# Gate and up products of layer 0's expert blocks as three rounded passes instead of one fp32 product

## The reference

```
combine = top-2 scores of the router, normed, zero for the other experts
for e in range(16):
    h = silu(flat @ Wu[e]) * (flat @ Wg[e])      # 256 -> 128
    out = out + combine[:, e:e+1] * (h @ Wd[e])  # 128 -> 256
out = out + silu(flat @ Su) * (flat @ Sg) @ Sd   # shared
```

## Time and profile before

| | us |
|---|---|
| median of 3 runs | 1170.13 |
| lowest, highest | 1168.87, 1175.76 |
| profiled execution | 1172.08 |
| its span, first to last instruction | 1169.5 |
| busy in the span: PE, DVE, ACT, POOL | 899.2, 685.6, 467.1, 621.2 |
| layer 0's dispatch, about | 297 to 364 |
| layer 0's 47 blocks, about | 364 to 452 |
| re-load and add of layer 0's results, about | 452 to 476 |

### The profile page before, as it was taken

One profiled execution on the slowest core, in us unless ns is written; L12 is line 12 of the kernel. 1 busy time (PEld: TensorE's weight loads), 2 busy tenths in 40 slices (PEclk: granted clock), 3 DMA queues, 4 the chain that ended last, 5 costly groups with the idle time before them and its releaser, 6 DMA issues.

```text
span 1169.5 us, 22075 instructions
## 1 busy us (share of the span) xinstructions
PE 899.2 (77%) x5927; PEld 691.8 (59%) x5927; DVE 685.6 (59%) x2692; ACT 467.1 (40%) x1176; POOL 621.2 (53%) x870
## 2 busy tenths in 40 slices
PE   1687989878597992379987888856899999989900
PEld 1465667657355881256665565533688887778700
DVE  4678888865532554467687674352455544444568
ACT  2346666743112441257655443311344444444400
POOL 3646666523163652336558888755356655545500
PEclk9859999988798996559989576787999999999955
DMA  8500000000624543400002222566455655545287
GB/s 231 192 2 1 2 2 1 1 2 1 263 106 127 152 130 120 144 1 2 2 29 86 85 97 101 210 222 221 147 163 174 182 157 161 153 141 156 70 327 319
DMA packets 73093, 136.97 MB, mean 117 GB/s; under 512 B 13406, under 2 KB 51725, under 8 KB 70928
## 3 DMA queue, kind: packets, MB, share of 16 engines
q1 hardware_dynamic: 52144, 85.15, 22.8%
q0 software_dynamic: 17632, 46.73, 11.2%
q10 hardware_dynamic: 3200, 3.70, 0.9%
HBM read 79.15 MB, written 62.39 MB: 121 GB/s over the span
## 4 chain that ended last, share of the span: by engine, by line
PE 36%; DVE 9%; POOL 6%; issue 5%; ACT 2%; another core or an unknown queue 1%; DMA 1%; DVEq 0%; POOLq 0%; ACTq 0%; SPq 0%
PE s_psum L1996 12%; PE s_psum L2009 6%; PE s_psum L1988 3%; POOL rows L1553 3%; PE s_psum L1477 3%; PE s_psum L2004 2%; DVE a_masked L1074 2%; DVE f_rows L2096 2%; DVE f_xT L2096 2%; PE s_psum L549 1%; POOL a_probs L1414 1%; PE s_psum L1496 1%; PE s_psum L646 1%; PE s_psum L602 1%
## 5 line engine op out<-in xcount | busy, mean ns | idle before, releaser
L2106 POOL DMA_INDIRECT parts<-e_y,e_dest x206 | 202.7, 984 | 180.7 <-DVE e_y L2079 96.9
L1996 PE MATMUL s_psum<-wres,e_xT 128*128 x824 | 213.9, 382 | 1.8 <-ACT e_xT L2036 1.0
L1996 PEld LDWEIGHTS s_psum<-wres,e_xT 128*128 128x128 f32 x824 | 156.1, 191 | 26.1 <-issue 5.4
L1414 POOL TENSOR_SCALAR_AFFINE_SELECT a_probs<-a_probs 128x256 f32<-128x256 f32 x256 | 107.5, 444 | 117.6 <-ACT a_probs L870 116.8
L1553 POOL DMA_INDIRECT rows<-f_rows,f_place_at x128 | 125.2, 978 | 40.3 <-issue 31.7
L2009 PE MATMUL s_psum<-wres,e_hT 128*128 x412 | 125.3, 386 | 12.2 <-ACT e_hT L2046 11.6
L870 ACT ACTIVATE a_probs<-s_psum 128x768 f32<-128x768 f32 x128 | 104.6, 817 | 72.8 <-PE s_psum L629 68.2
L2041 ACT ACTIVATE e_act_out<-s_psum 128x128 f32<-128x128 f32 x206 | 57.1, 277 | 180.8 <-PE s_psum L1996 101.6
L2070 DVE TENSOR_TENSOR e_hid<-e_act_out,s_psum 128x128 f32<-128x128 f32 x206 | 59.0, 286 | 91.8 <-issue 42.6
L1074 DVE CUSTOM_DVE_ANT_0 a_masked<-s_psum,a_ahead 128x128 f32<-128x128 f32 (+1 forms) x256 | 76.1, 353 | 42.0 <-PE s_psum L605 39.1
L2079 DVE TENSOR_SCALAR e_y<-s_psum,e_xg 128x256 f32<-128x256 f32 x206 | 99.6, 484 | 0.7 <-issue 0.7
(11 more groups left out here) (297 smaller groups left out, 1993.4 us busy)
## 6 DMA issues: line engine op xcount, KB each, us to landing
e_xg<-rows SPq DMA_DIRECT2D x159, 160.0 KB
f_rows<-parts SPq DMA_DIRECT2D x8, 1024.0 KB, 7.2
f_xT<-parts SPq DMA_DIRECT2D x8, 1024.0 KB, 7.4
wres<-in_experts SPq DMA_DIRECT2D x21, 384.0 KB
e_xg<-rows SPq DMA_DIRECT2D x47, 144.0 KB
wres<-in_experts SPq DMA_DIRECT2D x4, 1536.0 KB
rows<-empty SPq DMA_DIRECT2D x1, 5120.0 KB, 24.1
e_yk<-parts SPq DMA_DIRECT2D x16, 256.0 KB, 2.9
```

Of the source, the lines that this page charges most:

```text
L1414: last = nc.gpsimd.affine_select(out=diagonal[:, :, a], in_=diagonal[:, :, a], compare_op=ALU.is_ge, fill=0.0, base=0, pattern=[[0, 2], [1 ...
L1996: last = nc.tensor.matmul(ps_u[b % 2][:, 0:2 * P], xT[b % 2][:, c * P:(c + 1) * P], wres[:, ds(e, 1), 2 * c * P:2 * (c + 1) * P].rearrange ...
L2106: nc.gpsimd.indirect_dma_start(out=parts[:, :], out_offset=bass.IndirectOffsetOnAxis(ap=dest[b % NY][:], axis=0), in_=y[b % NY][:], in_off ...
```

## The change

It applies to layer 0 alone (`front is None`); layer 1's blocks keep their fp32 products.

- ScalarE rounds each quarter of the gate and up weights to fp32r (`up_hi`) after the Silu of shared units 0 to 3. VectorE subtracts this from the weights, in place in `wres` (`up_lo`), after the adds of units 0 to 3. TensorE's blocks wait for the four subtractions instead of the four transfers.
- ScalarE's copy `xT` is now rounded to fp32r. VectorE writes the remainder `xT_lo` from PSUM and `xT`, one more instruction a block.
- TensorE computes the gate and up product as three products of rounded parts, high with high, high with low, low with high, for each half of the width: six matmuls for two.
- The gathered rows and the results lie in the buffer from which the rows were scattered (`m_rows`) instead of buffers of their own.

```
+    up_hi = sb("up_hi", [P, E, D], F32R)
+    up_lo = wres[:, :, 0:D].bitcast(F32R)
...
 # dispatch, scalar
             nc.scalar.activation(act_out[i % 2][:], ps_a[i % 2][:], ACT.Silu).then_inc(act_done, 1)
+            if i < 4:
+                act.wait_ge(quarter_loaded[i], 16)
+                nc.scalar.activation(up_hi[:, parts4[i]], wres[:, parts4[i], 0:D], ACT.Copy).then_inc(up_hi_done, 1)
...
 # dispatch, vector, after the add of unit i
+            if i < 4:
+                dve.wait_ge(up_hi_done, i + 1)
+                nc.vector.tensor_tensor(up_lo[:, parts4[i]], wres[:, parts4[i], 0:D], up_hi[:, parts4[i]].bitcast(F32),
+                                        ALU.subtract).then_inc(up_lo_done, 1)
...
 # expert_blocks
+        if split:
+            sent = begun["rows"][:].rearrange("p t n -> p (t n)")
+            xg = [sent[:, i * RW:(i + 1) * RW] for i in range(NX)]
+            y = [sent[:, NX * RW + i * H:NX * RW + (i + 1) * H] for i in range(NY)]
...
             def up(b, e):
                 pe.wait_ge(xT_done, b + 1)
                 wait(pe, hid_done, b - 1)
+                if split:
+                    pe.wait_ge(xT_lo_done, b + 1)
+                    n = 0
+                    for c in range(FC):
+                        for rows_part, w in split_passes(xT[b % 2], xT_lo[b % 2], up_hi, up_lo):
+                            last = nc.tensor.matmul(ps_u[b % 2][:, 0:2 * P], rows_part[:, c * P:(c + 1) * P],
+                                                    w[:, ds(e, 1), 2 * c * P:2 * (c + 1) * P].rearrange("p a n -> p (a n)"),
+                                                    start=n == 0, stop=n == 3 * FC - 1)
+                            n += 1
+                    last.then_inc(u_ps, 1)
+                    return
...
+            def keep_x_lo(b):
+                dve.wait_ge(xT_done, b + 1)
+                wait(dve, u_ps, b - 1)
+                nc.vector.tensor_tensor(xT_lo[b % 2][:], ps_x[b % 2][:, 0:H], xT[b % 2][:].bitcast(F32),
+                                        ALU.subtract).then_inc(xT_lo_done, 1)
...
                     multiply(i)
+                if split and i + 2 < NB:
+                    keep_x_lo(i + 2)
```

More of the change, by code:

```diff
@@ L1602, in dispatch @@
     hid = [sb(f"hid{i}", [P, BLK]) for i in range(2)]
+    up_hi = sb("up_hi", [P, E, D], F32R)
+    up_lo = wres[:, :, 0:D].bitcast(F32R)
+    parts4 = [slice(q * E // 4, (q + 1) * E // 4) for q in range(4)]
     ps_a, ps_b = [psum[:, i] for i in range(2)], [psum[:, 2 + i] for i in range(2)]
@@ L1629, in dispatch @@
     chain = Chain(sem("chain"), 1000)
-    front = {"wres_loaded": wres_loaded, "wres_count": 64, "tab_done": tab_done, "scattered": scattered}
+    quarter_loaded = [sem(f"quarter_loaded{q}") for q in range(4)]
+    up_hi_done = sem("up_hi_done")
+    up_lo_done = sem("up_lo_done")
+    front = {"wres_loaded": up_lo_done, "wres_count": 4, "tab_done": tab_done, "scattered": scattered, "up_hi": up_hi,
+             "up_lo": up_lo, "rows": X}
     @block.sync
@@ L1634, in _ @@
         sp.dma_start(ws[:], w_shared.rearrange("h p n -> p h n")).then_inc(shared_loaded, 16)
-        for q in range(4):
-            part = slice(q * E // 4, (q + 1) * E // 4)
-            sp.dma_start(wres[:, part], w_all[part].rearrange("e p n -> p e n")).then_inc(wres_loaded, 16)
+        for part, landed in zip(parts4, quarter_loaded):
+            sp.dma_start(wres[:, part], w_all[part].rearrange("e p n -> p e n")).then_inc(landed, 16)
     @block.gpsimd
@@ L1930, in expert_blocks @@
         dest = [sb(f"dest{i}", [P, 1], I32) for i in range(NY)]
-        xT = [sb(f"xT{i}", [P, H]) for i in range(2)]
+        split = front is None
+        xT = [sb(f"xT{i}", [P, H], F32R if split else F32) for i in range(2)]
+        if split:
+            xT_lo = [sb(f"xT_lo{i}", [P, H], F32R) for i in range(2)]
+            up_hi, up_lo = begun["up_hi"], begun["up_lo"]
         act_out = [sb(f"act_out{i}", [P, P]) for i in range(2)]
@@ L1934, in expert_blocks @@
         hT = [sb(f"hT{i}", [P, P]) for i in range(2)]
-        y = [sb(f"y{i}", [P, H]) for i in range(NY)]
-        xg = [sb(f"xg{i}", [P, RW]) for i in range(NX)]
+        if split:
+            sent = begun["rows"][:].rearrange("p t n -> p (t n)")
+            xg = [sent[:, i * RW:(i + 1) * RW] for i in range(NX)]
+            y = [sent[:, NX * RW + i * H:NX * RW + (i + 1) * H] for i in range(NY)]
+        else:
+            y = [sb(f"y{i}", [P, H]) for i in range(NY)]
+            xg = [sb(f"xg{i}", [P, RW]) for i in range(NX)]
         if front is None:
@@ L1947, in expert_blocks @@
         xT_done = sem("xT_done")
+        xT_lo_done = sem("xT_lo_done")
         u_ps = sem("u_ps")
@@ L1985, in turn @@
                 loaded(pe, b)
+                if split:
+                    wait(pe, xT_lo_done, b - 1)
                 wait(pe, xT_done, b - 1)
@@ L2083, in _ @@
             dve.wait_ge(begun["tab_done"], 1)
+            if split:
+                keep_x_lo(0)
+                keep_x_lo(1)
             for i in range(NB + 2):
```

## The result

| | before | change |
|---|---|---|
| median, us | 1169.76 | 1187.93 |
| lowest, highest (4 runs each) | 1168.87, 1175.76 | 1181.91, 1191.51 |
| profiled execution; span | 1172.08; 1169.5 | 1187.08; 1185.3 |
| first to last of the 32 dispatch scatters | 42.9 | 49.3 |
| stretch of the blocks: first transposes to last weighed tile, layer 0 | 83.6 | 92.7 |

The table has one run of the kernel before more than the three of the earlier table; a stretch runs to the start of the last weighed tile. The change is slower: ratio 1.0175, 95% interval 1.0128 to 1.0222. The prediction (1169.4, range to 1178) was wrong. Its step on the dispatch scatters held up; its gain of 7 us in the blocks became a loss of 9.

A forecast was written before the change was run, and what follows sets the result against it. GpSimd's scatters were taken to set the time before layer 0's blocks, TensorE within them. Terms -7.2 + 0.3 + 6.2 = -0.7 us gave a median of 1169.4 us, range 1162 to 1178.

The forecast's parts named there:

- Gate and up products, -7.2 us: Layer 0's blocks: six single-pass matmuls take 0.714 instead of 0.866 us, 0.152 less a block, times 47 blocks.
- on the path: Layer 0's blocks: TensorE paces them, so the 7.2 us saved in gate and up products shortens the kernel.
- under 1.473: Layer 0's blocks: GpSimd's 1.30 us a scatter (0.98 plus 0.32 between) fits the new block period of 1.473 us.
- the 0.05 for other surprises: Rival on the whole kernel: matmuls not single-pass here, or other surprises such as idle time falling elsewhere; chance 0.05.
- Low part of the rows on VectorE, hidden: Layer 0's blocks: one more VectorE instruction, 0.42 us, hides in 0.43 and 0.28 us of waiting; first block +0.3 us.
- rival 3: Layer 0's blocks: VectorE paces them, period near 1.6 us, result 1175.4, or 1196.6 at the upper bound; chance 0.12.
- rival 2: Layer 0's blocks: TensorE's queue, slowed by address-setting instructions, becomes the bound; +4.1 instead of -7.2, result 1180.7 us; chance 0.08.
- Held scatters, +6.2: Dispatch before layer 0's blocks: each of four VectorE weight subtractions holds one GpSimd scatter, 1.55 us each; ends 0 and 8.8.
- the mean of 1.55: Dispatch: assumed hold per scatter in us, between 2.2 if it starts just inside a subtraction and 0.9 if one slipped through.
- Rival 1: Dispatch: scatters are not held, and blocks start when TensorE finishes the shared units at 366.4; result 1165.1 us; chance 0.25.
- Units of the shared expert, hidden: Before layer 0's blocks: TensorE starts 0.9 us late four times, units end at 366.4, hidden before first transposes at 370.7.
- Shared buffers, nothing: Layer 0: gathered rows and results in the old row buffer cost nothing, with same sizes and its scatters already waited for.

The follow-up runs named there:

- e16: Kernel before plus a GpSimd write of 128x464 zeros behind every result scatter of both layers' blocks; ratio 0.9909 to the kernel before, layer 0 stretch 80.8 us.
- e15: Blocks' half of the change alone, on unrounded loaded weights, with a result scatter for only every second block of layer 0; layer 0 stretch 73.6 us.
- e2_blocks: Blocks' half of the change alone: six fp32r matmuls and rows' remainders on the loaded weights, own buffers; ratio 1.0045 to the kernel before, layer 0 stretch 90.1 us.
- e5: Blocks' half of the change alone, without layer 0's result scatters, plain DMAs writing the results at the end; layer 0 stretch 73.4 us.
- e1_dispatch: Dispatch half of the change alone: weights rounded and subtracted, shared buffers, blocks still fp32 without remainders; ratio 1.0055 to the kernel before, layer 0 stretch 83.5 us.
- e4_wider: The change with each of the six matmuls 320 columns wide instead of 256; ratio 1.0118 to the kernel before, layer 0 stretch 86.0 us.
- e13: Kernel before plus a GpSimd write of 128x576 zeros behind every result scatter of both layers' blocks; ratio 1.0120 to the kernel before, layer 0 stretch 84.8 us.
- e14: The change plus a GpSimd write of 128x576 zeros behind every result scatter; ratio 1.0157 to the kernel before, layer 0 stretch 84.7 us.
- e17: The change plus a GpSimd write of 128x464 zeros behind every result scatter; ratio 0.9970 to the kernel before, layer 0 stretch 80.8 us.

## Why the prediction was wrong

- **Gate and up products, -7.2 us: the arithmetic right, the step wrong.** 0.12 us from start to start and 1.47 us a block came as forecast, where nothing was late. Where no stalls are in the way the difference is there too: 80.8 us regular at 1.62 (e16) against 73.6 at 1.47 (e15), 7.2 us. The failed step is the sentence that this lies "on the path" and that GpSimd's 1.30 us is "under 1.473". It priced a scatter by its busy time and gap, as if a scatter could follow another at 1.47 us and cost nothing. What the runs showed in its place: at 1.47 us and less between scatters TensorE's signals come late, and from 1.65 us on they do not. The earlier trace rows had the spacing, 0.98 + 0.64 = 1.62, between the two. In place of -7.2 the stage measured +6.5 (e2_blocks) and +9.1 (the change). None of the four rivals has this mechanism; only the 0.05 for other surprises covers it.
- **Low part of the rows on VectorE, hidden: right.** e5 and e15 have it and are regular at 1.47 us. So rival 3 is out, as is rival 2: no address instruction kept the second to the sixth matmul more than 0.12 us apart.
- **Held scatters, +6.2: right.** 49.3 - 42.9 = 6.4 in the change, 6.4 by e1_dispatch's ratio. The mechanism is the one forecast, but that the size came so near is in part luck. The held ones took 1.16 and three times 2.1 us longer, 7.5 us together and above the mean of 1.55 that I took. Against that the kernel before has one wait of 1.24 us between two scatters, 0.9 more than usual, which the change's trace does not have:
```profile
332.74 0.96 POOL L1647 DMA_INDIRECT rows<-m_rows,d_place_at  x1 [1.24 <-DMA rows<-m_rows,d_place_at]
```
Rival 1 is out. The Trainium skill (SBUF — State Buffer, Who interferes with whom) reports a probe in which a tensor_tensor did not stall such transfers; here four of four subtractions held one, 2.12 to 3.08 us against 0.96.
- **Units of the shared expert, hidden: right.** While the subtractions last, the units' `down` products start 6.11 us apart instead of 5.16, 0.95 more where 0.9 was forecast. The idle time before the last unit takes most of it up (1.92 us instead of 5.46), and TensorE stands 8.6 us idle behind them.
- **Shared buffers, nothing: right** (e1_dispatch).
- **The whole.** Halves alone cost 0.55% and 0.45%, together 1.0%; the change measured 1.0128 to 1.0222. Between 0.3% and 1.2% is not accounted for by either half. The change's stretch of 92.7 against e2's 90.1 is some of it, and layer 1's stretch alone varied from 270.2 to 281.8 between kernels that are the same there. In the two profiled executions the span grew by 15.8 us: 6.4 in the dispatch scatters and 9.1 in layer 0's blocks, and in stages that the change leaves alone +5.3 before the first scatter and -4.8 in layer 1's blocks. I leave the rest open.

**Shown and not shown.** Shown: result scatters 1.47 us apart or less bring the late signals, and a least spacing of 1.65 or 1.74 us, or one of mostly 2.9, takes them away; the scatters' bytes and rows, the loads, fp32r and VectorE's work do not bring them. Where between 1.47 and 1.65 the limit lies is not shown (one pair 1.54 us apart in e4_wider brought no late Silu). That it is the 1.56 us to the first packet is not shown either: in e16, behind 18 of 46 spacings, a scatter begins before the one ahead has sent its first packet, which comes up to 2.4 us after the begin, and no Silu is late. Not shown is also what the scatter and TensorE's signals share. In the stalls the recorded increments of TensorE's semaphores are 0.72 to 0.81 us apart and then come in a bunch (in the change at 430.95, 431.76, 432.48, 433.23, 433.32, 433.37, 433.40), close to the 0.74 us between GpSimd's wake-up and its scatter, and SyncE's next load is issued 0.4 us late at the same moments. It looks like a common way for writes that GpSimd occupies, but that is argued only. All times here are of recorded executions. The Trainium skill (NOTIFIC — the notification-queue block, 7.1 Overflow: three behaviours, one of which stalls the engine) describes a mode in which full record queues stall an engine; no run here can tell whether recording takes part. The kernel before goes wrong only after 28 blocks because only then do two of its scatters come close (412.40 and 413.71); what holds the first of them for 0.3 us is open. That stalls then go on fits the spacing: the blocks that catch up bring scatters 1.29 us apart. With 1.65 as the least (e16) the late Silus are gone in layer 0 (7 before) and in layer 1 (38 before), where 6 steps of 158 stay irregular instead of 63. The same holds in e13, e14 and e17: none has a late Silu in either layer.

## What to carry to other kernels

Before making an engine's work shorter in a loop, ask for each other engine how closely its steps may follow each other. Its busy time does not tell: here it said 1.30 us, and the loop had to keep more than 1.47. A loop that runs just above such a limit looks as if it were bound by its busiest engine. When a reader of an engine's result is late though the engine's rows show no gap, try the loop at a slower pace: a short filler on the queue that collides can be worth more than a faster matmul.

## What the runs showed of the hardware

- Indirect scatters on GpSimd, 128 rows of 1 KB: 0.98 us recorded, first packet mostly 1.56 to 1.57 us after the begin and up to 2.4 us (e16_spaced_464); 64 rows still 0.91 us recorded.
- Result scatters begun 1.21 to 1.47 us apart are followed by Silus that TensorE's semaphore releases up to 3.3 us late, also at a granted clock of 1.0; with at least 1.65 us between them in both layers (e13, e14, e16, e17) none is late.
- A VectorE tensor_tensor with both inputs in SBUF (128x2048) holds a dispatch scatter that begins inside it: 2.12 to 3.08 against 0.96 us, four times of four.
- fp32r matmuls of 256 columns with a weight load each: 117 to 120 ns from start to start within a group of six.
- GpSimd's memset of 128 rows: 0.292 us for 192 columns, 0.521 for 464, 0.615 for 576.
